# Delta-rule attention with a soft mixture of experts: the weights' preparation and the first maxima regrouped in the first passes, and the low weights turned three tiles ahead in the combination

## The reference

```python
# 4 sequences of 2048 tokens, 256 wide; C = 128; 1024 slots (8 experts x 128), hidden 1024
x = x + attn(layernorm(x))
x = x + ffn(layernorm(x))

def attn(x):                                  # gated delta rule, token by token
    q, k, v = x @ Wq + bq, x @ Wk + bk, x @ Wv + bv
    k = k / norm(k)
    alpha, beta, gate = sigmoid(x @ Wa + ba), sigmoid(x @ Wb + bb), sigmoid(x @ Wg + bg)
    S = S @ (alpha * (I - beta * k k^T)) + beta * v k^T
    o = (q @ S) * gate
    return o @ Wo + bo

def ffn(x):                                   # soft mixture of experts
    xn, se = rms_norm(x, gamma_x), rms_norm(slot_embeds, gamma_slot)
    logits = xn @ se^T                        # 2048 x 1024 a sequence
    slots = softmax(logits, over tokens)^T @ xn
    processed = gelu(slots @ w1) @ w2
    return softmax(logits, over slots) @ processed
```

## Time and profile before

| what | value |
| --- | --- |
| median of 3 runs | 1190.32 us (1187.75 to 1190.52) |
| profiled execution, its own time | 1187.25 us |
| its span, from first to last instruction | 1185.4 us |
| TensorE busy | 1113.2 us (94%), 8600 matmuls |
| VectorE busy | 938.2 us (79%) |
| ScalarE busy | 735.6 us (62%) |
| GpSimd busy | 314.5 us (27%) |
| mean granted TensorE clock | 0.985 |

### The profile page before, as it was taken

One profiled execution on the slowest core, in us unless ns is written; L12 is line 12 of the kernel. 1 busy time (PEld: TensorE's weight loads), 2 busy tenths in 40 slices (PEclk: granted clock), 3 DMA queues, 4 the chain that ended last, 5 costly groups with the idle time before them and its releaser, 6 DMA issues.

```text
span 1185.4 us, 26905 instructions
## 1 busy us (share of the span) xinstructions
PE 1113.2 (94%) x8600; PEld 854.5 (72%) x8600; DVE 938.2 (79%) x2195; ACT 735.6 (62%) x1385; POOL 314.5 (27%) x389
## 2 busy tenths in 40 slices
PE   4489999999999889899999999999999999999998
PEld 2378888888888764587786486787486787487787
DVE  4789888888889747997586898576898666998665
ACT  3446567665766445687663697664587664497763
POOL 3647656676567611000021000022000022000012
PEclk9699999999999989999999999999999999999999
DMA  6113432233233343232273031264031355000155
GB/s 191 45 45 81 125 98 85 87 107 119 80 88 95 99 96 100 66 72 57 55 170 78 2 72 45 63 147 103 2 72 32 74 123 130 0 1 1 22 119 128
DMA packets 185519, 94.02 MB, mean 79 GB/s; under 512 B 123680, under 2 KB 176928, under 8 KB 185440
## 3 DMA queue, kind: packets, MB, share of 16 engines
q1 hardware_dynamic: 178384, 75.40, 26.6%
q0 software_dynamic: 5792, 17.05, 4.9%
q10 hardware_dynamic: 1264, 0.53, 0.2%
HBM read 38.42 MB, written 29.36 MB: 57 GB/s over the span
## 4 chain that ended last, share of the span: by engine, by line
PE 66%; DVE 16%; issue 11%; ACT 4%; POOL 2%; DMA 1%; DVEq 1%; SPq 0%; ACTq 0%; POOLq 0%
PE m_wide L2015 14%; PE m_wide L1992 7%; PE m_wide L1978 7%; PE m_wide L1898 6%; PE a_bank L1095 4%; DVE m_Dm L1598 3%; PE a_bank L1107 3%; PE a_bank L1157 2%; DVE m_El L1606 2%; PE m_wide L2003 2%; ACT m_Eh L1781 2%; PE a_bank L1233 2%; PE a_bank L1146 2%; DVE cmax L1569 2%; PE m_wide L1952 2%
## 5 line engine op out<-in xcount | busy, mean ns | idle before, releaser
L1536 POOL DMA_DIRECT2D out_dram<-m_o x64 | 35.4, 553 | 627.1 <-DVE m_o L1720 514.3
L1952 PE MATMUL m_wide<-m_X,m_Eh 128*128 128x257 f16 (+1 forms) x1024 | 171.5, 273 | 2.7 <-DVE m_El L1606 2.7
L1898 PE MATMUL m_wide<-seT,XT 128*128 128x512 f16 x672 | 147.3, 379 | 0.9 <-issue 0.8
L2015 PE MATMUL m_wide<-m_Ph,m_Th 128*128 128x257 f16 x512 | 140.4, 274 | 4.3 <-DVE m_Pl L1645 4.3
L1952 PE MATMUL m_wide<-m_X,m_El 128*128 128x257 f16 (+1 forms) x512 | 139.7, 273 | 0.0
L2015 PE MATMUL m_wide<-m_Ph,m_Tl 128*128 128x257 f16 x512 | 139.4, 272 | 0.0
L2015 PE MATMUL m_wide<-m_Pl,m_Th 128*128 128x257 f16 x512 | 139.1, 272 | 0.0
L1898 PEld LDWEIGHTS m_wide<-seT,XT 128*128 (+1 forms) x672 | 65.5, 98 | 78.5 <-ACT L L1754 1.5
L1952 PEld LDWEIGHTS m_wide<-m_X,m_Eh 128*128 128x128 f16 x1024 | 99.2, 98 | 20.8 <-DVE m_El L1606 3.8
L1754 ACT COPY L<-m_wide 128x512 f32<-128x512 f32 (+1 forms) x112 | 65.1, 584 | 78.6 <-PE m_wide L1898 77.8
L1774 ACT ACTIVATE m_E<-m_Dm,m_eshift 128x512 f32<-128x512 f32 x128 | 92.5, 722 | 23.5 <-DVE m_Dm L1598 22.5
(11 more groups left out here) (198 smaller groups left out, 2712.5 us busy)
## 6 DMA issues: line engine op xcount, KB each, us to landing
L<-in_L_attn_x_dram SPq DMA_DIRECT2D x16, 512.0 KB, 7.2
Mrep<-M_dram SPq DMA_DIRECT2D x32, 256.0 KB
x_dram<-x SPq DMA_DIRECT2D x16, 512.0 KB, 6.6
m_X<-X_dram SPq DMA_DIRECT2D x128, 64.0 KB, 1.8
m_x1t<-x_dram POOLq DMA_DIRECT2D x32, 256.0 KB, 3.5
out_dram<-m_o POOLq DMA_DIRECT2D x64, 128.0 KB, 2.4
M_dram<-M_ SPq DMA_DIRECT2D x16, 256.0 KB, 2.6
X_dram<-Xh SPq DMA_DIRECT2D x16, 256.0 KB, 2.3
```

Of the source, the lines that this page charges most:

```text
L1898: last = pe.matmul(lg[t % 4], XT[:, sx * KD + k, bass.ds((4 * g + t) * P, P)], seT[:, ss, k, z * HS:(z + 1) * HS], start=(c == 0), stop=(c ...
L1952: last = pe.matmul(acc[v][q], e[t % 4][:, qs], X[:, sx, bass.ds(4 * g + t, 1), 0:XW].rearrange("q a n -> q (a n)"), start=first and e is E ...
L2015: last = pe.matmul(co[p], a, pp[:, e, 0:XW], start=(c == 0), stop=(c == 3 * NS - 1))
```

## The change

Six things are done together.

1. *Combination.* TensorE turns tile 2 ahead of the loop as well, and in the loop tile n+3 behind the products of tile n.
2. *Passage.* VectorE's memset of cmax and the maxima of tiles 0 and 1 go into step 14, those of tiles 2 to 5 into step 15.
3. *Low half of w2.* GpSimd makes it at the end of step -3, ahead of the slot norms, in two operations (scale in place, subtract); VectorE's L706 is gone.
4. *Step -2.* GpSimd does key norms and beta ahead of the cuts; TensorE turns the keys and makes the system ahead of the first turn of Z, and ScalarE copies the keys first. VectorE's cast of w1 moves from the head of the step to behind the decays.
5. *Slots.* VectorE scales them in step -2, four on either side of the first doubling, no longer at the head of step -1. The high half goes to ScalarE in step 0, the low half stays on VectorE, in step 1. The low half of w1 moves to step -1. For that w1 is scaled in the room of the slots' halves.
6. VectorE's and ScalarE's steps 0 and 1 are unrolled.

```diff
         slots_g = room_of_L(1, NS * D).rearrange("p (e d) -> p e d", e=NS)
-        sp_h, sp_l = [room_of_L(1, NS * D // 2).bitcast(F16).rearrange("p (e d) -> p e d", e=NS) for n in range(2)]
+        sp_room = room_of_L(1, NS * D)
+        sp_h, sp_l = [sp_room[:, n * NS * D // 2:(n + 1) * NS * D // 2].bitcast(F16)
+                      .rearrange("p (e d) -> p e d", e=NS) for n in range(2)]
         sn2 = sb("sn2", [P, NS])
...
-        w1_g = slots_g[:, :, :].rearrange("p e d -> p (e d)").rearrange("p (k n) -> p k n", k=KD)
+        w1_g = sp_room.rearrange("p (k n) -> p k n", k=KD)
...
                 at = i if isinstance(i, int) else None
+                if at == -2:
+                    if live(i + 3):
+                        key_norms(i + 3)
                 if live(i + 2):
                     residual(i + 2, q)
+                if at == -2:
+                    if live(i + 3):
+                        spread_beta(i + 3)
                 if live(i + 2):
...
                     output_norm(i)
-                if live(i + 3):
+                if live(i + 3) and at != -2:
                     key_norms(i + 3)
...
                     spread_blocks(i + 2, q)
-                if live(i + 3):
+                if live(i + 3) and at != -2:
                     spread_beta(i + 3)
...
                 if at == -3:
+                    second_weights_low()
                     slot_norms()
+            def second_weights_low():
+                pool.wait_ge(w2h_ok, 1)
+                pool.tensor_scalar(w2_in, w2_in, WSCALE, None, ALU.mult).then_inc(w2h_ok, 1)
+                pool.wait_ge(w2h_ok, 2)
+                pool.tensor_tensor(w2s[:, 1, :, :], w2_in, w2s[:, 0, :, :], ALU.subtract).then_inc(w2h_ok, 1)
             def slot_norms():
...
                     dve.tensor_copy(w1s[:, 0, :, :], w1_g).then_inc(w1_ok, 1)
-                elif step == 4:
-                    dve.wait_ge(w2h_ok, 1)
-                    dve.scalar_tensor_tensor(w2s[:, 1, :, :], w2_in, WSCALE, w2s[:, 0, :, :],
-                                             ALU.mult, ALU.subtract)
                 elif step == 5:
...
-            def slots_scaled():
-                dve.wait_ge(srn_ok, 1)
-                dve.wait_ge(w1_ok, 3)
-                dve.wait_ge(gxs_ok, 1)
-                for e in range(NS):
+            def slots_scaled(first, past):
+                if first == 0:
+                    dve.wait_ge(srn_ok, 1)
+                    dve.wait_ge(w2h_ok, 3)
+                    dve.wait_ge(gxs_ok, 1)
+                for e in range(first, past):
                     last = dve.scalar_tensor_tensor(slots_g[:, e, :], slots_in[:, e, :], srn[:, e:e + 1], gxs[:, :],
                                                     ALU.mult, ALU.mult)
-                last.then_inc(slots_ok, 1)
-            def slots_high():
-                dve.wait_ge(slots_ok, 1)
-                dve.tensor_copy(sp_h[:, :, :], slots_g[:, :, :]).then_inc(slots_ok, 1)
+                if past == NS:
+                    last.then_inc(slots_ok, 1)
...
                         biases(i + 3, r, 1)
-                    mixture_weights(3)
-                    mixture_weights(4)
-                if at == -1:
-                    slots_scaled()
-                    slots_high()
                 for s in range(BS - 1):
...
                             weights(i + 1, r)
+                        if at == NCH - 2:
+                            early_maxima(0)
                     if s == 10:
...
                             gated(i + 1, r)
+                        if at == NCH - 2:
+                            early_maxima(1)
                 if live(i + 2):
...
                     mixture_weights(2)
+                if at == -2:
+                    mixture_weights(3)
                 if live(i + 3):
...
                     decays_from_start(i + 3, r, 0)
+                if at == -2:
+                    slots_scaled(0, NS // 2)
                 if live(i + 2):
...
                 if at == -2:
-                    mixture_weights(5)
+                    slots_scaled(NS // 2, NS)
                 if at == -1:
+                    mixture_weights(5)
+                if at == 1:
                     slots_low()
                 if at == NCH - 1:
-                    for t in range(3):
+                    for t in range(2, 6):
                         early_maxima(t)
...
-            steps(dve, step)
-            for t in range(3, NT):
+            steps(dve, step, first=1)
+            for t in range(6, NT):
                 early_maxima(t)
...
                 for e in range(NS):
-                    last = act.activation(sp_h[:, e, :], slots_in[:, e, :], ACT.Square, accum_out=sn2[:, e:e + 1])
+                    last = act.activation(slots_g[:, e, :], slots_in[:, e, :], ACT.Square, accum_out=sn2[:, e:e + 1])
                 last.then_inc(sq_ok, 1)
+            def slots_high():
+                act.wait_ge(slots_ok, 1)
+                act.wait_ge(w1_ok, 3)
+                act.copy(sp_h[:, :, :], slots_g[:, :, :]).then_inc(slots_ok, 1)
             def turned_slots(es):
...
                     keys(i + 3, r)
+                if at == 0:
+                    slots_high()
                 if live(i + 3):
                     gates(i + 3, r)
+                if at == -2:
+                    if live(i + 3):
+                        turned_keys(i + 3)
                 if live(i + 2):
...
                     turned_slots((0,))
-                if live(i + 3):
+                if live(i + 3) and at != -2:
                     turned_keys(i + 3)
...
                 act.sem_inc(L_ok[p], 2)
-            steps(act, step)
+            steps(act, step, first=1)
             for t in range(8, NT):
...
                     spread_alpha(i + 3)
+                if at == -2:
+                    if live(i + 3):
+                        turn_keys(i + 3, r)
+                if at == -2:
+                    if live(i + 3):
+                        system(i + 3)
                 if live(i + 2):
...
                     turn_slots((0,))
-                if live(i + 3):
+                if live(i + 3) and at != -2:
                     turn_keys(i + 3, r)
...
                     turn_slots((1,))
-                if live(i + 3):
+                if live(i + 3) and at != -2:
                     system(i + 3)
...
                 turn(0, 1)
+                turn(0, 2)
                 cut_to = value(pe, nb * QS + 1)
...
                         combine(k, t)
-                        turn(k + (t + 2) // 4, (t + 2) % 4)
+                        turn(k + (t + 3) // 4, (t + 3) % 4)
                 for t in range(4):
                     combine(QB - 1, t)
-                    if t < 2:
-                        turn(QB - 1, t + 2)
+                    if t < 1:
+                        turn(QB - 1, t + 3)
 
```

More of the change, by code:

```diff
@@ L812, in step @@
                 if at == -2:
+                    slots_scaled(NS // 2, NS)
+                if at == -1:
                     mixture_weights(5)
-                if at == -1:
+                if at == 1:
                     slots_low()
                 if at == NCH - 1:
-                    for t in range(3):
+                    for t in range(2, 6):
                         early_maxima(t)
```

## The result

The change makes the kernel slightly slower: a median of 1191.62 us (1190.14 to 1194.80, 15 runs) against 1187.94 (1185.35 to 1190.53, 15 runs of the kernel before beside it), a ratio of 1.0031, 95% interval 1.0021 to 1.0041. The forecast had been no change, within 0.3%. The profiled execution took 1194.80 us with a span of 1193.2, the slowest of the 15; its span is 7.8 us above that of before, twice what the medians differ by. So the two traces show places, and the sizes come from timed kernels.

The account below looks back on a forecast made before the run. TensorE was taken to bound first passes and combination, other engines mattering only where it waits. +0.3 - 2.6 - 2.3 + 1.4 + 3.2 = 0.0 us left the forecast median at 1190.3 us, range 1183.5 to 1195.0.

Parts of the forecast that it names:

- the combination's +0.3 us: Combination, four batches: waits of 0.52 us against 0.45 gained per batch, +0.3 us in all.
- three turns per batch wait 0.20, 0.16 and 0.16: Combination: in each batch three TensorE turns wait for their low part Wl, 0.52 us together.
- the margin of 0.16 for tile 6: Combination: tile 6's Wl ready at 598.46, its turn wanted at 598.62, so in time by 0.16 us.
- The gain ahead of the products, 0.45: Combination: tile 2's turn fills TensorE's idle time before the first products, so 0.45 us per batch leave the full stretch.
- The second rival: Combination: every turn waits for its Wl, 13 turns in 4 batches by 0.13 us; +4.7, 1195.0 us, chance 0.12.
- The passage, -2.6: First passes to mixture: TensorE's waits for cmax and column maxima go, X's transfers then bind, dispatch begins 2.6 us earlier.
- The wait for X: Ahead of the dispatch: TensorE waits 0.3 to 1 us for X, whose transfers nothing moves.
- Start and steps 0 and 1, together +2.3: Steps -2 and -1 gain 2.3 us, step 0 costs 1.4, step 1 costs 3.2.
- the first rival: Step -2: the port lock spares the slots, second doubling 4.7 us sooner; -4.7, 1185.6 us, chance 0.28.
- Step 0: ScalarE's cast of the slots between keys and gates delays TensorE's products: +1.4 us, bounds 0 and 2.0.
- Step 1: VectorE's low half of the slots ahead of Xl makes the second doubling 3.2 us late: +3.2, bounds 1.7 and 4.8.
- the fall of the clock: Step 1: the granted clock may fall, taking its cost to 4.8 us; 0.03 chance of leaving the 0.3% band.

Follow-up runs that it names:

- run 1: Kernel before with the change to the combination alone (turns three tiles ahead): 1193.38 against 1189.99 us, ratio 1.0028.
- run 2: Kernel before with the combination's change, same work order, but the loop's jump moved behind products: 1189.69 against 1189.99 us, ratio 0.9994.
- run 3: Kernel before with only tile 2's turn moved ahead of the first products, later turns two tiles ahead, jump behind products: 1187.27 against 1188.87 us, ratio 0.9985.
- run 5: Kernel before with the change to the start and steps 0 and 1 alone: 1189.90 against 1189.99 us, ratio 1.0003.
- run 4: The whole change, but turns after tile 2's run two tiles ahead, with the jump behind products: 1184.54 against 1187.78 us for the kernel before, ratio 0.9966.
- run 10: Kernel before with only VectorE's and ScalarE's steps 0 and 1 written out: 1193.60 against 1188.44 us, ratio 1.0039.
- run 8: Kernel before with the change to the passage alone: 1184.29 against 1188.87 us, ratio 0.9956.
- runs 6: Kernel before with the start's change, slots' low half in four pieces, two in step 1, two in step 12: 1184.01 against 1189.99 us, ratio 0.9946.
- the variant: Best combined kernel, but the slots' low half as one two-slot operation in each of steps 0 to 3: 1180.45 us, ratio 0.9928 to the kernel before.

## Why the prediction was wrong, and where it was right

**The step that failed is the combination's +0.3 us.** Alone it measured +3.3, which is the whole of the change's +3.7 within the intervals. Two things in it were wrong. First, "the others are in time" and "three turns per batch wait 0.20, 0.16 and 0.16": in run 1 the right three wait, but 0.27, 0.25 and 0.25 in batch 0 (in run 2, where nothing else is late: 0.28, 0.25, 0.24). The hop, which I took as 0.1, is 0.19 in the row of tile 4 there (Wl ends at 595.90, the turn starts at 596.09). That is 0.25 us more per batch; only in batch 3 did the three wait less than I had said, 0.09 each. In the change the margin of 0.16 for tile 6 was gone as well in batch 0. Second, and larger, I had no term for the loop's end: of the 3.6 us in the trace of run 1 it makes 2.8, the waits 2.6, and the turn of tile 2 gives back 1.8. I asked whether the turns are in time, not how long ahead of its products a turn is released. Before, a turn was free long ahead, and its products followed in 3.10 us at every loop end; that TensorE's queue had run past it and through the jump is my reading of that. Now it is released just as it is wanted, and behind it only the eight transposes, 0.45 us, cover the jump to the next iteration. Run 2, with the same order of work and the jump behind 2.65 us of products, removes it. The gain ahead of the products, 0.45, came as forecast (run 3: 0.46).

The second rival put the combination at +5.0 us (6.8 less the 1.8 gained), nearer to the +3.3 than the sum was. That is luck: its mechanism, a wait at all 13 turns, is not what the traces show.

**The passage, -2.6, was right** in kind. In size it is near in the traces (3.0 us alone, 2.6 in the change against run 5, from the logits to the first products), but timed alone it gave -5.2 us (-7.1 to -3.2), twice the term. Of the 3.0 us the dispatch has 1.4, counted from step 13; the 1.6 behind the dispatch I had not counted. The wait for X is there (1.84, not 0.3 to 1). In the change itself it is not. I had said that nothing moves X, but with the later steps its transfers come later too (issued from 474.85 to 498.42, the last ones starting before 499.50), and the logits end at 500.32. In run 4 they end at 499.98, and TensorE waits 0.82 us.

**Start and steps 0 and 1, together +2.3, measured +0.4** (-1.1 to +1.8) **and the terms erred both ways.** The slots are spread over 8.6 us in place of 3.24, as the sum had them, so the first rival falls. The exclusive lock of the port pair, as "SBUF — State Buffer" of the Trainium skill (SBUF: two separate sides) has it, agrees with that. GpSimd's pair took 9.45 us, and its scaling with a single input 5.38 of them, above my bound of 5.1; it cost nothing, for the columns began at 36.73 all the same. My estimate of some 9 us from the price in "GPSIMD Engine Reference" of the Trainium skill (section 3.1) was near. The first columns of steps -1, 0 and 1 came at 71.88, 96.37 and 121.56 (72.4, 97.1, 123.3 said), that of step 2 at 150.98 (150.7 said). The last is luck: step 0 was cheaper and step 1 dearer than their terms. Step 0 was dearer by 0.37, not 1.4: run 10, with the same steps written out and no cast, has it at 24.63, so the cast itself costs 0.56, within my bounds. Step 1 was mis-sized, +5.2 against +3.2. I gave the fall of the clock 0.03 of chance and only 4.8 us, though the sum had the doubling 3.2 late with TensorE idle for it, near the 3.87 that already stood before a stretch at half rate. The slowdown ran on into step 2 as well, which I left out. Of what brought the start back to nothing 2.7 us lie in the mixture; the rest is no more than two executions of one kernel differ by.

The parts do not add up: 0.28, -0.44 and 0.03% make -0.13%, and the change measured +0.31%. The traces place part of the 5 us between them. From dispatch to products, over four batches, runs 1, 8 and 5 take 0.7, 1.6 and 1.6 us less than before, the change only 1.8; the 1.6 of run 8 came with the wait for X, which the change has not. The logits behind batches 0 and 1 take 1.4 more than before, while the three runs make +0.3 together. That comes with TensorE's program: run 4, which differs in nothing else, has them 1.0 under before, and TensorE's idle time at the jump back is 0.39 there and 1.66 in the change. Why that jump takes longer in the change and in run 1 stays open. So does what in the placement of ScalarE's code delays it in run 10.

## What to carry to other kernels

Before you let an engine's queue wait nearer to its due time, ask what comes behind the wait: a loop's jump needs queued work in front of it, and a wait that is "just in time" takes that away. Put the jump behind the longest work of the body; here that was worth 3.7 us with the order of the work unchanged. Put a long operation of a side job into the places where its engine waits anyway, in pieces; one piece of 2.4 us cost step 1 twice its length.

## What was not expected of the hardware

- The end of a loop of three iterations cost TensorE 0.32, 0.31 and 0.09 us (run 1, batch 0) where a wait that ended just then and only 0.45 us of work stood ahead of it. It cost nothing behind the same 0.45 us released long before (the kernel before), and nothing behind 2.65 us of work (run 2).
- The granted clock fell to 1.2 GHz behind 3.08 and 2.02 us of idle time in a busy stretch, not behind 1.07, and behind 1.47 in one execution of two of the same kernel.
- Writing out two steps on VectorE and ScalarE made the unchanged code behind them 2.6 us slower at each of two jumps back of the outer loop. "Runtime: NRT & Kernel Launch" of the Trainium skill (Instruction fetch mechanics) says that a taken branch out of the loaded window has to fetch its target first. ScalarE's idle time at the jump, 4.38 us instead of 1.19, fits that; no run here shows the window.
- The step in which VectorE or ScalarE enters its loop takes 0.7 to 0.9 us more, and the place moves with the loop's start: step 0 before (TensorE enters there too), step 2 in runs 6 and 10, steps 2 and 4 in the variant.
